# A graph-transformer kernel on one core: degree counts by comparison sums, node projection reordered, one-hots in 16 bits

## The reference, cut to what matters

```
# layer 0, on xn = layernorm(x): the inputs of the attention over edges and of the linear mixer
q, k, v      = xn @ Wq + bq, xn @ Wk + bk, xn @ Wv + bv
mq, mk, mv   = split(xn @ W_qkv + b_qkv, 3)
k2           = normalised square of (mk - mean(mk)); q2 likewise of mq
kv           = k2^T @ mv                    # 256 x 256, summed over all nodes
# layer 1: mean of the neighbours
seg_sum = segment_sum(nodes[senders], receivers)
counts  = segment_sum(ones, receivers)
h_neigh = seg_sum / maximum(counts, 1)
# layer 1, gated experts: 131072 other, unsorted edges with their own counts per node
```

## Time and profile before

| | us |
|---|---|
| median of three runs | 10104.04 |
| the profiled execution | 10101.38 |
| its span | 10099.8 |
| `project_nodes`, until its last copies | 25 to 831 |
| `plan_steps` | 831 to 891 |
| `attention_output` | 3506 to 3889 |
| `neighbour_sums` | 5757 to 8010 |
| busy over the span: PE, DVE, ACT, POOL | 6612.7, 4971.5, 3047.8, 6028.1 |

### The profile page before, as it was taken

How to read it: one execution, slowest core, us unless ns; L and a number is a source line. 1 busy time by engine, 2 the same in 40 slices (tenths; PEclk the granted TensorE clock), 3 DMA queues, 4 the chain that set the end, 5 groups by cost and what they waited for, 6 DMA issues and landing times. The chain is left out here.

```text
span 10099.8 us, 132193 instructions
## 1 busy us (share of the span) xinstructions
PE 6612.7 (65%) x29670; PEld 5007.3 (50%) x29671; DVE 4971.5 (49%) x10855; ACT 3047.8 (30%) x7313; POOL 6028.1 (60%) x6341
## 2 busy tenths in 40 slices
PE   4664898989889875886888555554444554555530
PEld 2333666666666664775777344443333443333320
DVE  6874777777777777665566311111111222222224
ACT  1112656666666411111222033333333211111110
POOL 1223666666666402777777377777777527777762
PEclk8777999999999997776888777777776767777765
DMA  2114766767777523222666344443333322222214
GB/s 75 50 55 156 211 206 208 209 207 209 208 209 209 168 84 99 79 79 70 179 177 176 96 120 119 119 119 101 100 101 100 87 69 44 45 44 44 44 29 159
DMA packets 657561, 1228.04 MB, mean 122 GB/s; under 512 B 165550, under 2 KB 409474, under 8 KB 657253
## 3 DMA queue, kind: packets, MB, share of 16 engines
q0 software_dynamic: 301872, 718.92, 25.9%
q1 hardware_dynamic: 327959, 467.65, 14.9%
q10 hardware_dynamic: 27580, 39.79, 1.1%
HBM read 1088.88 MB, written 145.05 MB: 122 GB/s over the span
## 5 line engine op out<-in xcount | busy, mean ns | idle before, releaser
L948 POOL DMA_INDIRECT e_kv<-KV,e_idx x1712 | 1629.4, 952 | 760.7 <-issue 483.4
L2469 POOL DMA_INDIRECT s_x<-XN,s_idx x1712 | 1621.3, 947 | 589.7 <-issue 500.8
L2526 PE MATMUL s_psA<-s_x,s_oh 128*128 128x256 f32 x1712 | 664.4, 477 | 1112.7 <-DMA s_x<-XN,s_idx 1022.1
L1593 POOL DMA_INDIRECT SD<-o_pay,o_pos x1024 | 1077.9, 1053 | 360.3 <-issue 314.6
L2884 POOL DMA_INDIRECT t_g<-G,t_idx x1088 | 1076.1, 989 | 329.6 <-issue 329.6
L2562 DVE TENSOR_TENSOR NS<-s_psA,NS 128x256 f32 x856 | 363.7, 425 | 1743.3 <-PE s_psA L2527 1742.9
L1053 PE MATMUL e_psQ<-QA,e_oht 128*128 x3424 | 893.7, 407 | 200.7 <-issue 115.8
L2526 PEld LDWEIGHTS s_psA<-s_x,s_oh 128*128 128x128 f32 x1712 | 405.9, 245 | 1222.7 <-issue 1152.5
L1053 PEld LDWEIGHTS e_psQ<-QA,e_oht 128*128 128x128 f32 x3424 | 646.7, 199 | 367.8 <-issue 281.4
L3052 PE MATMUL t_psH<-t_xT,t_w 128*128 128x384 f32 (+1 forms) x1088 | 425.4, 558 | 378.8 <-ACT t_H L3029 358.2
L988 ACT ACTIVATE QA<-e_psA 128x264 f32 x856 | 332.0, 388 | 996.1 <-PE e_psA L1073 986.2
(11 more groups left out here) (580 smaller groups left out, 12424.9 us busy)
## 6 DMA issues: line engine op xcount, KB each, us to landing
o_dbf<-DBF SPq DMA_DIRECT2D x128, 512.0 KB
f_w<-in_L_ffn_Wd_dram SPq DMA_DIRECT2D x57, 1024.0 KB
e_relb<-REL SPq DMA_DIRECT2D x107, 512.0 KB, 5.9
o_dlo<-DLO SPq DMA_DIRECT2D x128, 256.0 KB
e_kv<-KV,e_idx POOLq DMA_INDIRECT x1712, 3.8
s_x<-XN,s_idx POOLq DMA_INDIRECT x1712, 2.8
YD<-t_y ACTq DMA_DIRECT2D x50, 512.0 KB, 2.7
mx_y<-YD SPq DMA_DIRECT2D x10, 2560.0 KB, 12.4
```

The lines of the kernel that those rows point to most:

```text
L948: pool.indirect_dma_start(kv[:, s, t, :], None, k.KV, bass.IndirectOffsetOnAxis(ap=idx[:, s, t:t + 1], axis=0)).then_inc(kv_in[s][g], 16)
L1593: pool.indirect_dma_start(self.k.SD, bass.IndirectOffsetOnAxis(ap=self.pos[:, s, j:j + 1], axis=0), self.pay[:, s, j, :], None).then_inc(s ...
L2469: pool.indirect_dma_start(x[:, s, t, :], None, k.XN2, bass.IndirectOffsetOnAxis(ap=idx[:, s, t:t + 1], axis=0)).then_inc(x_in[s], 16)
L2526: pe.matmul(psA[:, u % 4, 0:C], oh[:, o, 2 * u, :], x[:, s, 2 * u, :], start=True, stop=False)
```

## The change

**Counting.** `LaneLists` is replaced by `WindowCounts`. The edge list is turned into float32 once; for each tile t one DVE instruction compares all 1612 edges of each partition with the number 128(t+1), writes the results as bfloat16 and adds them up into a column of `below`. The total over the partitions is the number of edges below the window's end, which `plan_steps` uses where it had a running sum. The number of edges of each node, needed in the second layer, comes out of `neighbour_sums`: each gathered row gets a 257th column of ones.

**Projection reordered.** The statistics and the normalised rows are made two tiles ahead, inside `tail` of tile t. The first bank of `psP` has a semaphore of its own in both directions, `allp` is split into `qrow` and a double `mixp`, and the loads, roots and stores are ordered to suit.

**Second count in 16 bits.** `GatCount` compares bfloat16 with bfloat16. The table's edge index is made the innermost one, so that TensorE reads columns that lie 16 elements (32 bytes) apart.

The diff, cut:

```diff
         pool.memset(self.k.dsti[:], N).then_inc(self.set_done, 1)
-
-
...
+    def convert(self, dve):
+        dve.wait_ge(self.set_done, 2)
         dve.wait_ge(self.in_done, 32)
-        link(dve.tensor_scalar(self.lo_i[:], k.dsti[:], P - 1, None, ALU.bitwise_and))
-        link(dve.tensor_scalar(self.hi_i[:], k.dsti[:], 7, None, ALU.logical_shift_right))
-        link(dve.tensor_copy(self.lo[:], self.lo_i[:]))
-        link(dve.tensor_copy(self.hi[:], self.hi_i[:]))
-
...
-        last.then_inc(self.counted, 1)
+        dve.tensor_copy(self.dstf[:], self.k.dsti[:]).then_inc(self.ready, 1)
+        dve.tensor_copy(self.lim[:], self.lim_i[:]).then_inc(self.ready, 1)
+        dve.wait_ge(self.ready, 2)
+
+    def count(self, dve, t):
+        dve.tensor_scalar(self.inside[:], self.dstf[:], self.lim[:, bass.ds(t, 1)], None, ALU.is_lt, ALU.add,
+                          accum_out=self.k.below[:, bass.ds(t, 1)]).then_inc(self.ready, 1)
 
 
...
-        allp = sb("allp", [P, W3])
+        qrow, mixp = sb("qrow", [P, C]), sb("mixp", [P, 2, 3 * C])
...
+        def pairs(eng, body):
+            with eng.Fori(0, NT // 2 - 1) as j:
+                body(2 * j, 0, True)
+                body(2 * j + 1, 1, True)
+            body(NT - 2, 0, False)
+            body(NT - 1, 1, False)
...
             def store(t, s):
                 after(sp, evac_done, t)
-                sp.dma_start(rows(k.Q, t), allp[:, 0:C]).then_inc(stored_q, 16)
+                sp.dma_start(rows(k.Q, t), qrow[:]).then_inc(stored_q, 16)
                 sp.dma_start(rows(k.KV, t), kvrow[:]).then_inc(stored_kv, 16)
-                sp.dma_start(rows(k.MV, t)[:, C:2 * C], allp[:, 5 * C:6 * C]).then_inc(stored_m, 16)
+                sp.dma_start(rows(k.MV, t)[:, C:2 * C], mixp[:, s, 2 * C:3 * C]).then_inc(stored_v, 16)
                 after(sp, q2_done, t)
-                sp.dma_start(rows(k.MV, t)[:, 0:C], q2[:]).then_inc(stored_m, 16)
+                sp.dma_start(rows(k.MV, t)[:, 0:C], q2[:]).then_inc(stored_q2, 16)
...
-            def head(t, s):
-                after(pool, xn_done, t - 2)
+            def load(t, s):
                 pool.dma_start(xt[:, s, :], rows(k.XP, t)).then_inc(x_in[s], 16)
+
+            def root(t):
                 after(pool, var_ready, t)
                 pool.tensor_tensor(rstd[:], ve[:], k.neghalf[:], ALU.pow).then_inc(rstd_ready, 1)
 
-            def tail(t, s):
+            def body(t, s, more):
+                if more:
+                    after(pool, xn_done, t + 1)
+                    load(t + 3, 1 - s)
                 after(pool, sq_done, t)
                 pool.tensor_tensor(q4[:], q4s[:], k.half[:], ALU.pow).then_inc(q4_done, 1)
-            skewed(pool, head, tail)
+                if more:
+                    root(t + 2)
+            load(0, 0)
+            load(1, 1)
+            counts.pad(pool)
+            root(0)
+            after(pool, xn_done, 0)
+            load(2, 0)
+            root(1)
+            with pool.Fori(0, NT // 2 - 2) as j:
+                body(2 * j, 0, True)
+                body(2 * j + 1, 1, True)
+            body(NT - 4, 0, True)
+            after(pool, sq_done, NT - 3)
+            pool.tensor_tensor(q4[:], q4s[:], k.half[:], ALU.pow).then_inc(q4_done, 1)
+            root(NT - 1)
+            body(NT - 2, 0, False)
+            body(NT - 1, 1, False)
             pool.wait_ge(norm_sb, 1)
             pool.tensor_tensor(cr[:], cn[:], k.half[:].to_broadcast([P, KC]), ALU.pow).then_inc(root_done, 1)
...
-            def head(t, s, fill):
-                def between():
-                    fill(0)
-                    after(dve, xT_ps, t - 1)
+            def stats(t, s):
                 ln.start(t)
                 loaded(dve, x_in[s], t, s)
-                layernorm_dve(dve, ln, xt[:, s, :], xn[:], st, mv, ve, rstd, var_ready, rstd_ready, xn_done, t, between)
+                after(dve, xn_done, t - 1)
+                ln(dve.bn_stats(st[:], xt[:, s, :]))
+                ln(dve.bn_aggr(mv[:], st[:]))
+                dve.tensor_scalar(ve[:], mv[:, 1:2], LN_EPS, None, ALU.add).then_inc(var_ready, 1)
                 ln.end()
 
-            def tail(t, s, fill):
+            def normed(t, s):
+                after(dve, xT_ps, t - 1)
+                after(dve, rstd_ready, t)
+                dve.tensor_scalar(xn[:], xt[:, s, :], mv[:, 0:1], rstd[:, 0:1], ALU.subtract, ALU.mult).then_inc(xn_done, 1)
+
+            def tail(t, s, more):
                 mix.start(t)
                 after_dma(dve, stored_q, t - 1)
                 after_dma(dve, stored_kv, t - 1)
-                after_dma(dve, stored_m, t - 1, 2)
-                after(dve, acc_done, t - 1)
+                after_dma(dve, stored_v, t - 1)
+                after(dve, acc_done, t - 2)
+                flat = psP[:].rearrange("p a n -> p (a n)")
+                after(dve, first_done, t)
+                dve.tensor_tensor(qrow[:], flat[:, 0:C], bcat[:, 0:C], ALU.add)
+                dve.tensor_tensor(kvrow[:, 0:C], flat[:, C:2 * C], bcat[:, C:2 * C], ALU.add).then_inc(first_free, 1)
                 after(dve, proj_done, t)
-                flat = psP[:].rearrange("p a n -> p (a n)")
-                dve.tensor_tensor(allp[:, 0:C], flat[:, 0:C], bcat[:, 0:C], ALU.add)
-                dve.tensor_tensor(kvrow[:, 0:C], flat[:, C:2 * C], bcat[:, C:2 * C], ALU.add)
+                dve.tensor_tensor(mixp[:, s, :], flat[:, 3 * C:W3], bcat[:, 3 * C:W3], ALU.add)
                 dve.tensor_tensor(kvrow[:, C:KW].rearrange("p (h d) -> p h d", h=HEADS)[:, :, 0:DK],
                                   flat[:, 2 * C:3 * C].rearrange("p (h d) -> p h d", h=HEADS),
-                                  bcat[:, 2 * C:3 * C].rearrange("p (h d) -> p h d", h=HEADS), ALU.add)
-                dve.tensor_tensor(allp[:, 3 * C:W3], flat[:, 3 * C:W3], bcat[:, 3 * C:W3], ALU.add).then_inc(evac_done, 1)
+                                  bcat[:, 2 * C:3 * C].rearrange("p (h d) -> p h d", h=HEADS), ALU.add).then_inc(evac_done, 1)
                 after(dve, evac_done, t)
-                mix(dve.tensor_reduce(mean[:], allp[:, 3 * C:5 * C].rearrange("p (a n) -> p a n", a=2), AX.X, ALU.add))
+                mix(dve.tensor_reduce(mean[:], mixp[:, s, 0:2 * C].rearrange("p (a n) -> p a n", a=2), AX.X, ALU.add))
                 dve.tensor_scalar(nmean[:], mean[:], -1.0 / C, None, ALU.mult).then_inc(mean_done, 1)
-                fill(1)
+                if more:
+                    stats(t + 2, s)
+                counts.count(dve, t)
                 after(dve, sq_done, t)
                 mix(dve.tensor_scalar(s2e[:], s2[:], 1e-7, None, ALU.add))
                 mix(dve.reciprocal(r2[:], s2e[:]))
+                after(dve, acc_done, t - 1)
                 dve.tensor_scalar(k2[:], sq[:, 1, :], r2[:, 1:2], k.valid[:, bass.ds(t, 1)], ALU.mult, ALU.mult)\
                     .then_inc(k2_done, 1)
-                fill(2)
                 after(dve, q4_done, t)
 
                 mix(dve.tensor_scalar(qn[:], q4[:], r2[:, 0:1], 1e-12, ALU.mult, ALU.max))
                 mix(dve.reciprocal(qr[:], qn[:]))
                 mix(dve.tensor_scalar(qn[:], qr[:], r2[:, 0:1], None, ALU.mult))
+                after_dma(dve, stored_q2, t - 1)
                 dve.tensor_scalar(q2[:], sq[:, 0, :], qn[:, 0:1], None, ALU.mult).then_inc(q2_done, 1)
                 after(dve, k2_done, t)
                 after(dve, q2_done, t)
                 mix.end()
+                if more:
+                    normed(t + 2, s)
+            stats(0, 0)
+            normed(0, 0)
...
-            lists.dve_start(dve)
-            beside(dve, head, tail, lists.dve_step)
-            lists.dve_end(dve)
+            stats(1, 1)
+            normed(1, 1)
+            counts.convert(dve)
+            pairs(dve, tail)
+            dve.wait_ge(counts.ready, 2 + NT)
...
                 after(pe, xT_sb, t)
-                after(pe, evac_done, t - 1)
+                after(pe, first_free, t - 1)
                 for g in range(3):
+                    if g == 1:
+                        after(pe, evac_done, t - 1)
                     for a in range(KC):
                         last = pe.matmul(psP[:, g, :], xT[:, a, :], wcat[:, a, g * 512:(g + 1) * 512],
                                          start=(a == 0), stop=(a == KC - 1))
+                    if g == 0:
+                        last.then_inc(first_done, 1)
                 last.then_inc(proj_done, 1)
 
-            def tail(t, s, fill):
+            def tail(t, s):
                 after(pe, k4_done, t)
...
                 after(pe, k4_done, t)
                 after(pe, k2_done, t)
                 for a in range(KC):
-
-                    pe.matmul(psK[:, a, :], allp[:, 5 * C + a * P:5 * C + (a + 1) * P], k2[:],
...
-            pe.matmul(psA[:, 0:NT], k.ones[:], k.cnt[:], start=True, stop=True).then_inc(summed, 1)
```

(55 more changed lines are left out.)

84 lines of the change are left out of this document (15 added, 69 removed).

## The result

| | before | after |
|---|---|---|
| median of the runs, us | 10104.35 (4 runs) | 9752.15 (4 runs) |
| ratio after / before | | 0.9647, interval 0.963 to 0.9663 |
| the profiled execution, and its span | 10101.38, 10099.8 | 9736.01, 9734.4 |

A forecast was written before the change was run, and what follows sets the result against it. The prediction took DVE to bound `project_nodes`, neither DVE nor TensorE full in `attention_output`'s loop, POOL's gathers `neighbour_sums`; -243 and -33 on 10101.4 gave 9825, plus 2.7 for the median 9828, range 9755 to 9920.

The forecast's parts named there:

- the tile of 10.2 us: `project_nodes`: DVE's time per tile after the change, 8.0 kept plus 0.3 for waits plus 1.9 for the count.
- the loop at 12.0: `attention_output`: TensorE's own work, 9.2 plus 2 x 1.4 per pair of tiles, decides the loop; -18 us.
- DVE sets `project_nodes`; the count takes 1.9: `project_nodes`: DVE bounds the loop, and the added comparison of 1612 elements with a sum takes 1.9 us per tile.
- Start at 70.4: `project_nodes`: the first `tail` starts at 70.4 us, 1.0 for a conversion and 0.4 for small steps after the edge list.
- rival 1: `project_nodes`: the count runs two elements a cycle, DVE's tile is 9.3, `kvT` 45 us earlier; total 9783; chance 0.20.
- DVE idles more than 1 us per tile: `project_nodes`: a sign in the profile after the change that would show the prediction wrong.
- TensorE's clock above 0.85: `project_nodes`: the loop's granted clock after the change exceeds 0.85, with projection entries 0.43 us apart.
- rival 2: `project_nodes`: TensorE's clock stays at 1.2 GHz for most of the loop, tile 14.0 us; total 10014; chance 0.15.
- Second count: 1.9 on DVE, 0.13 per strided pair: `attention_output`: DVE's comparison block falls from 3.5 to 1.9 us; TensorE's strided load and matmul pair takes 0.13 us.
- Rival 4: `attention_output`: TensorE's step costs 0.21 us a pair, +51 us instead of -33; total 9912; chance 0.05.
- Rival 3: `attention_output`: 16-bit comparisons run at the old pace, the block stays 3.5 us; total 9864; chance 0.08.
- The chain through the load at 11.1: `attention_output`: the chain from DVE's L1478 through the `xt` load to TensorE and back falls from 12.7 to 11.1 us.

## Why the prediction was right and wrong, step by step

The prediction went out of its range by two steps together, the tile of 10.2 us and the loop at 12.0: the first missed 49 us, the second 31, and either alone would have left the time inside.

- **DVE sets `project_nodes`; the count takes 1.9.** Right: 1891 ns, and the 48 us of the added comparison. One of the two rows behind it was misread, without effect: L276 has an int32 source, not a float32 one.
- **Start at 70.4.** 1.9 too early: the list landed 1.4 later, and 0.85 us pass between the conversion's end and the first copy. The end, 9.3 instead of 11.0 behind the last L453, pays that back.
- **A tile of 10.2. This step failed**, by 1.0 us in each of 49 tiles, all of the 49 us. I read the earlier trace rows's 0.61 us between L212 and L453 as six waits at 0.1 and booked four more, +0.3. It was mostly one wait, for DVE's own result, which the change drops: 0.49 (the run with it put back). The booked 0.3 is hardly there either: with the wait back the tile is 9.67, of which all but the count (1.82) is 7.85, no more than the 8.0 read before. The last 0.2 lie in two readings. The next instruction starts 1.82 us behind the count's start (298.76 to 300.58), not 1.9. And the 8.0 held waits of the comparison blocks, which went with them: from `ve` (L209, below) to the block at 204.86 0.28 pass, from `ve` (L407) to the count 0.15.

```profile
204.58 0.15 DVE L209 TENSOR_SCALAR ve<-mv 128x1 f32<-128x1 f32 x1
```

- **9.19 is near rival 1's 9.3** by accident: rival 1 wanted a count of 1.0, and the count takes 1.89.
- **The sign "DVE idles more than 1 us per tile"** was set badly. It came, with 1.85 us per tile, but before it was 2.3: most of this is short idle time between small instructions, which the 8.0 held already.
- **TensorE's clock above 0.85.** Right, 0.93, and rival 2 falls. With more work taken off DVE it is 1.00.
- **Second count: 1.9 on DVE, 0.13 per strided pair.** Both came out to a hundredth. The 0.13 was luck: the row it came from (DVE's L483) has nothing to do with TensorE. Rival 4's 0.21 was far off. Rival 3 falls with L1389's 1227 ns.
- **The loop at 12.0 per pair of tiles. The term was mis-sized**: 10.46 came out, -49 us instead of -18. I took TensorE's own work, 9.2 per pair, from a stretch with pauses in it and a granted clock of 0.90, then filled the pauses in. Without its blocks of 0.7 that is 9.2 - 1.4 = 7.8. In the changed loop the clock is 0.99, and the same work takes 2 x (5.23 - 2.13) = 6.2, with 2.13 for a block: 1.6 less per pair of tiles, some 39 us in 25 pairs. Of these 1.6 the output product (L1531, after the change L1516) has 1.1: its three groups take 460, 447 and 407 ns an entry before, 384 or 385 after. Some 6 of them go back, because the old pairs were 2 x 6.23 = 12.5 us apart and not 12.7: my 317 us reached beyond the 25 pairs. The 0.90 stood beside the 230 in the earlier trace rows.
- **The chain through the load at 11.1** was too high as well: with two edges innermost it shows itself at 10.1.
- **The blocks behind the loop**: -17 against -18. **Neighbour sums, plan**: 0 as said (2244.3 us against 2245.5; from `kvT` to the first gather of `edge_attention` 71.4 against 72.1).

Both misses have one form: a duration that belonged to the old schedule (a stall behind a wait, work at a slow clock) was carried into the new one as if it were a property of the instructions.

## What to carry to other kernels

When a stage is costed anew, take busy times at the clock that the new schedule will have, and split every idle stretch between what an instruction costs and what waits for a result that the new order no longer asks for. Work placed in a wait for another engine is free until that wait is full; the next microsecond costs nearly its whole length, and taking work out again gives back only what stuck out. Before paying for a stride on one engine to gain pace on another, look for a layout with a short innermost run: it served both here.
